# Adding the two halves of an attention accumulator before the scale instead of after it

## The reference, cut to what matters

```python
xf = x.reshape(B, C, N)
f = einsum('kc,bcn->bkn', w1, xf) + b1[None, :, None]     # 16 rows
energy = einsum('bkn,bkm->bnm', f, f)
attention = softmax(energy, axis=-1)
out = einsum('bcm,bnm->bcn', xf, attention)
x = x + out.reshape(B, C, H, W) * 0.1                     # layer 0
...
a = binary_act(x); bw = binarize_weights(weights)         # layer 1
y = conv(a, bw, padding 1)
x = (y - mean) * rsqrt(var + eps) * gamma + beta + x
```

## Time and profile before

| | |
|---|---|
| median of 3 runs | 2013.26 us (2013.1 to 2013.76) |
| the profiled execution | 2013.64 us, its span 2011.8 us (1.84 us lie around it) |
| TensorE busy | 95% |
| DVE, ACT, Pool busy | 80%, 71%, 59% |
| attention, conv | about 54 to 1777 us; 1790.7 us to the end |

### The profile page before, as it was taken

How to read it: one execution, slowest core, us unless ns; L and a number is a source line. 1 busy time by engine, 2 the same in 40 slices (tenths; PEclk the granted TensorE clock), 3 DMA queues, 4 the chain that set the end, 5 groups by cost and what they waited for, 6 DMA issues and landing times. The chain is left out here.

```text
span 2011.8 us, 40245 instructions
## 1 busy us (share of the span) xinstructions
PE 1921.0 (95%) x15232; PEld 1655.3 (82%) x15232; DVE 1600.5 (80%) x2145; ACT 1425.8 (71%) x2794; POOL 1185.0 (59%) x849
## 2 busy tenths in 40 slices
PE   6999999999999999999999999999999999979990
PEld 2799899998889889998899989989999999844440
DVE  6777888888887888888788888888888887647778
ACT  5777777778777777778777777787777777633326
POOL 4555555558755555668655555577555556277750
PEclk7899999999999999999999999999999999989995
DMA  6111101012111111122111110111101102442019
GB/s 215 35 50 60 58 32 40 26 63 73 56 47 60 60 39 31 32 74 93 58 53 60 35 40 22 56 56 53 32 29 31 31 30 76 158 162 110 0 42 375
DMA packets 58279, 133.55 MB, mean 66 GB/s; under 512 B 9329, under 2 KB 9329, under 8 KB 57585
## 3 DMA queue, kind: packets, MB, share of 16 engines
q1 hardware_dynamic: 58096, 131.10, 19.2%
HBM read 84.48 MB, written 33.62 MB: 59 GB/s over the span
## 5 line engine op out<-in xcount | busy, mean ns | idle before, releaser
L724 POOL CAST Ph<-P 128x1024 fp32r<-128x1024 f32 x496 | 715.3, 1442 | 655.6 <-ACT P L497 655.6
L590 DVE TENSOR_REDUCE nb<-scw 128x1 f32<-128x512 f32 (+1 forms) x988 | 680.7, 689 | 271.3 <-PE scw L399 264.4
L508 ACT ACTIVATE scw<-scw,nb 128x512 f32<-128x512 f32 (+1 forms) x988 | 656.1, 664 | 338.1 <-DVE nb L590 337.9
L417 PE MATMUL accb<-Ph,xh 64*128 64x512 f32 x2048 | 809.5, 395 | 1.4 <-ACT tb L518 1.3
L417 PE MATMUL acct<-Ph,xh 64*128 64x512 f32 x2048 | 807.3, 394 | 0.0
L417 PE MATMUL accb<-Ph,xl 64*128 64x512 f32 x2048 | 801.2, 391 | 0.0
L417 PE MATMUL acct<-Ph,xl 64*128 64x512 f32 x2048 | 796.4, 389 | 0.0
L600 DVE TENSOR_TENSOR Pl<-P,Ph 128x1024 fp32r<-128x1024 f32 x512 | 671.9, 1312 | 23.5 <-ACT Ph L502 17.8
L417 PE MATMUL acct<-Pl,xh 64*128 64x512 f32 x2048 | 635.4, 390 | 0.0
L417 PE MATMUL accb<-Pl,xh 64*128 64x512 f32 x2048 | 632.5, 388 | 0.0
L497 ACT ACTIVATE P<-ee 128x1024 f32<-128x1024 f32 x512 | 526.2, 1028 | 64.2 <-PE ee L390 39.4
(11 more groups left out here) (120 smaller groups left out, 1391.0 us busy)
## 6 DMA issues: line engine op xcount, KB each, us to landing
wk<-xt SPq DMA_DIRECT2D x32, 512.0 KB, 3.8
xres<-x SPq DMA_DIRECT2D x32, 512.0 KB, 3.9
x<-xres SPq DMA_DIRECT2D x32, 512.0 KB, 2.8
R<-rd SPq DMA_DIRECT2D x32, 256.0 KB, 3.2
xn<-x SPq DMA_DIRECT2D x16, 512.0 KB, 11.8
xr<-x SPq DMA_DIRECT2D x16, 512.0 KB, 11.2
out<-xr SPq DMA_DIRECT2D x16, 512.0 KB, 3.4
An<-x SPq DMA_DIRECT2D x14, 512.0 KB, 5.0
```

The costliest lines, as they stand in the source:

```text
L417: return pe.matmul(to[:, :], w[rows, g * GM + k, c * 128:(c + 1) * 128], p[rows, s, k * QC:(k + 1) * QC], start=g == 0 and i == 0, stop=g ...
L508: nc.scalar.activation(to, to, ACT.Exp, bias=nb[:, t % 2, w:w + 1], accum_out=bsum[:, t % 2, w:w + 1]).then_inc(bsum_done, 1)
L590: nc.vector.tensor_reduce(nb[:, t % 2, w:w + 1], of, AX.X, ALU.max, negate=True).then_inc(nmax_done, 1)
L724: nc.gpsimd.tensor_copy(Ph[:, e % RP, :], P[:, e % 2, :]).then_inc(ph_done, 1)
```

## The change

For each chunk and half c, ACT still copies `acc_b` to `tb`. DVE now waits for that copy, adds it to `acc_t` straight from PSUM and writes the sum to `tc` (`join`, in the place of `scale_top`). Pool then multiplies `tc` by R once (`scale`) and adds it to x (`add_x`): four Pool operations to a chunk where there were six, at steps 1, 4, 8, 12 (or 2, 5, 11, 13). The waits follow: DVE's operation no longer waits for R but for ACT's copy and, before it overwrites `tc`, for `add_x` of the chunk before; ACT's copy, before it overwrites `tb`, waits for DVE's operation of the chunk before instead of `add_x`; the load of R waits for the two scales only.

```diff
@@ -299,7 +298,6 @@
             def load_r(t):
                 sp.wait_ge(rd_out, 64 * (t + 1))
                 if t >= 1:
-                    sp.wait_ge(top_done, CT * t)
                     sp.wait_ge(scaled, CT * t)
                 sp.dma_start(R[:], rd.rearrange("(o n) -> o n", o=1).to_broadcast([128, QC])).then_inc(r_in, 16)
 
@@ -514,7 +512,7 @@
                 else:
                     act.wait_ge(av_done, 2 * G * (t + 1))
                 if t > 0:
-                    act.wait_ge(x2_done, CT * (t - 1) + c + 1)
+                    act.wait_ge(top_done, CT * (t - 1) + c + 1)
                 nc.scalar.copy(tb[:, c, :], acc_b[c][:]).then_inc(bot_done, 1)
 
             def copy_f(s, bank):
@@ -600,15 +598,15 @@
                 nc.vector.tensor_tensor(Pl[:, e % RP, :], P[:, e % 2, :], Ph[:, e % RP, :].bitcast(F32),
                                         ALU.subtract).then_inc(pl_done, 1)
 
-            def scale_top(t, c):
-                dve.wait_ge(r_in, 16 * (t + 1))
+            def join(t, c):
+                dve.wait_ge(bot_done, CT * t + c + 1)
                 if c == 0:
                     dve.wait_ge(acc_done, 2 * (t + 1))
                 else:
                     dve.wait_ge(av_done, 2 * G * (t + 1))
                 if t > 0:
-                    dve.wait_ge(joined, CT * (t - 1) + c + 1)
-                nc.vector.tensor_tensor(tc[:, c, :], acc_t[c][:], R[:], ALU.mult).then_inc(top_done, 1)
+                    dve.wait_ge(x2_done, CT * (t - 1) + c + 1)
+                nc.vector.tensor_tensor(tc[:, c, :], acc_t[c][:], tb[:, c, :], ALU.add).then_inc(top_done, 1)
 
             def row_max(t):
                 dve.wait_ge(nmax_done, unit_count(SU * (t + 1) - 1))
@@ -672,7 +670,7 @@
                 for s in HEAD_HL.get(u, ()):
                     split_f(s)
                 if g == 0 and t >= 1:
-                    scale_top(t - 1, 1)
+                    join(t - 1, 1)
                 if u < UH:
                     block_max(2 * u, wide[u % 3][:])
                 elif u < NG:
@@ -680,7 +678,7 @@
                 if 0 <= e - 1 < NG:
                     lower(e - 1)
                 if g == G - 1 and t >= 0:
-                    scale_top(t, 0)
+                    join(t, 0)
                 if UH <= u < NG:
                     block_max(2 * u + 1, sc[1])
                 if g == 7 and 0 <= t + 1 < NT:
@@ -698,7 +696,7 @@
                     c = g
                     nc.vector.tensor_reduce(al[:, c:c + 1], xn[:, c, 0:TAPS * C], AX.X, ALU.add,
                                             apply_absolute_value=True).then_inc(al_done, 1)
-            scale_top(NT - 1, 1)
+            join(NT - 1, 1)
 
         @block.gpsimd
         def _(pool):
@@ -723,20 +721,15 @@
                     pool.wait_ge(av_done, 2 * (e - RP + 1))
                 nc.gpsimd.tensor_copy(Ph[:, e % RP, :], P[:, e % 2, :]).then_inc(ph_done, 1)
 
-            def scale_bottom(t, c):
+            def scale(t, c):
                 pool.wait_ge(r_in, 16 * (t + 1))
-                pool.wait_ge(bot_done, CT * t + c + 1)
-                nc.gpsimd.tensor_tensor(tb[:, c, :], tb[:, c, :], R[:], ALU.mult).then_inc(scaled, 1)
-
-            def join(t, c):
+                pool.wait_ge(top_done, CT * t + c + 1)
+                nc.gpsimd.tensor_tensor(tc[:, c, :], tc[:, c, :], R[:], ALU.mult).then_inc(scaled, 1)
+
+            def add_x(t, c):
                 pool.wait_ge(scaled, CT * t + c + 1)
-                pool.wait_ge(top_done, CT * t + c + 1)
-                nc.gpsimd.tensor_tensor(tb[:, c, :], tb[:, c, :], tc[:, c, :], ALU.add).then_inc(joined, 1)
-
-            def add_x(t, c):
-                pool.wait_ge(joined, CT * t + c + 1)
                 pool.wait_ge(xres_in[t % 2], 16 * (t // 2 + 1))
-                nc.gpsimd.tensor_tensor(xres[:, t % 2, c, :], tb[:, c, :], xres[:, t % 2, c, :],
+                nc.gpsimd.tensor_tensor(xres[:, t % 2, c, :], tc[:, c, :], xres[:, t % 2, c, :],
                                         ALU.add).then_inc(x2_done, 1)
 
             for h in range(2 * XG):
@@ -748,13 +741,11 @@
                     round_p(e)
                 part = None
                 if t >= 1:
-                    part = {k: i for i, k in enumerate((2, 5, 8, 11, 13, 15) if t % CH == 0 else (1, 3, 6, 9, 12, 15))}.get(g)
+                    part = {k: i for i, k in enumerate((2, 5, 11, 13) if t % CH == 0 else (1, 4, 8, 12))}.get(g)
                 if part in (0, 1):
-                    scale_bottom(t - 1, part)
-                if part in (2, 4):
-                    join(t - 1, part // 4)
-                if part in (3, 5):
-                    add_x(t - 1, part // 5)
+                    scale(t - 1, part)
+                if part in (2, 3):
+                    add_x(t - 1, part - 2)
                 h = split_at(*divmod(n - 1, G))
                 if h is not None:
                     lower_x(h)
@@ -767,8 +758,7 @@
                     pool.wait_ge(signed, CT * (k + 1))
                     transform_unit(nc, pads[k], V[k], v_done)
             for c in range(CT):
-                scale_bottom(NT - 1, c)
-                join(NT - 1, c)
+                scale(NT - 1, c)
                 add_x(NT - 1, c)
 
 
```

More of the change, by code:

```diff
@@ L177, in attention @@
         scaled = sem("scaled")
-        joined = sem("joined")
         e_done = sem("e_done")
```

## The result

The changed kernel takes 2050.14 us (median of 4 runs, 2048.16 to 2051.55), the kernel before 2013.18 in the same comparison: a ratio of 1.0183, 95% interval 1.0165 to 1.0201. The profiled execution took 2050.09 us, its span is 2048.2, 36.4 longer than the span before.

A forecast was written before the change was run, and what follows sets the result against it. TensorE, 95% busy, was taken as the bound, losing time only where made to wait. The terms 30.6 + 16.2 - 8.5 - 3.9 = +34.4 us gave a forecast of 2048 us, range 2026 to 2063.

The forecast's parts named there:

- The joins: At 30 chunk ends, DVE's joins wait for ACT's copies, so TensorE starts c = 1 1.02 us later: +30.6 us.
- What is late next: In step 1, `lower` behind the second join overlaps Pool's cast, delaying TensorE's second scan 0.54 us, 30 times: +16.2 us.
- the replay: Chunk 9's end retimed with the joins, using gaps from the profile; `lower` starts 0.27 us inside Pool's cast.
- Pool: `add_x` of c = 0 moves from step 9 to 8, ending step 11's wait: 23 chunks times 0.37, -8.5 us.
- The tail: After the last attention matmul, Pool runs four operations instead of seven before the convolution: -3.9 us.
- The clock: Clock taken as 1.00; its rival: idling at each boundary sets off a clock fall, 62 us more, 2110 us, chance 0.02.
- the other rivals: Step 1's wait absent, 2031 us (0.16); step 2 also delayed, 2063 (0.10); step 11 keeps its wait, 2056 (0.06).
- the not-slower case: Joins covered beside TensorE's first half step, only gains stay: 2001 us, chance 0.07; faster below 0.41 us a boundary.

The follow-up runs named there:

- the three kernels with the maximum moved: Step 15's `block_max` put ahead of DVE's c = 0 operation: changed kernel 2016.43 us; also `lower` ahead of second join 2003.33; kernel before, `add_x` in steps 8 and 14, 2004.69.
- the wait-alone run: Kernel before, with only a wait added so that DVE's `scale_top` also waits for ACT's copy: 2062.04 us, ratio 1.0242.

## Why the prediction was right, point by point

The forecast was 2048, the measurement 2050.1.

- **The joins** (+30.6 forecast, +25.6 measured). The mechanism is as told, and adding the wait alone makes it. The size was 0.2 us a boundary too large, in two places. ACT's second copy starts 0.67 after the start of its sum, not the 0.78 that I took from the earlier trace rows: there the sum's accumulator read was followed by nothing, since the copy waited for Pool. And TensorE restarts 0.06 after the join's end (618.33 to 618.39), not 0.14. One sign did not come: the gap ahead of c = 1 was to be near 1.3 us, 1.42 from the scan's start to the matmul's, and is 0.94. Part of the wait lies ahead of c = 0 instead, which the prediction took as hidden inside this wait. That is right for the sum, since the start of c = 1 hangs on the second join alone (0.06 behind its end at every boundary), but it made me miss what was left when that wait was taken away (the three kernels with the maximum moved).
- **What is late next** (+16.2 forecast, +17.7 measured). `lower` starts 0.25 inside the cast where the replay said 0.27, and is held to 1.08 behind its end. Moving `lower` ahead takes this term away and nothing else of its size; that the overlap alone makes it is worked out from the rows, not run. In the Trainium skill, SBUF — State Buffer, section "SBUF: two separate sides", GpSimd and a VectorE operation with two SBUF inputs take a pair of ports in turn, for a whole instruction; the 1.87 us here and the 1254 ns of the tiny operation with `add_x` in step 9 agree with that.
- **Pool** (-8.5 forecast, -9.7 measured). Step 11 is free, in nearly all chunks; one number in Pool's list gives it and takes it away, in either kernel. What I costed at nothing, the Pool parts that now fall into steps which also split x (chunks 7, 15, 23), came to 2.1 us in steps 7 and 8.
- **The tail** (-3.9 forecast, -3.9 measured): four operations, and the convolution's first matmul 17.87 us behind the last energy matmuls instead of 21.77. No run varied it by itself.
- **The clock.** The mean from 60 to 1740 us is 1.00, with waits of TensorE's weight loads up to 1.5 us and of its matmuls up to 1.1 in the list: no fall, so that rival is out. It is a mean: the first stretch, 60 to 64 us, still shows 0.50, but that is in chunk 0, ahead of every boundary.
- The terms come to +29.6 where +34.4 was forecast. That the total is close all the same is luck: some 7 us lie elsewhere, which the prediction had put at nothing, 4.6 of them in the steps named above and the rest in chunk 0 and in tenths that no run here isolates.
- Of the other rivals, the not-slower case stands against the wait-alone run. Its point, 0.41 us a boundary, was right in kind: with `lower` and the maximum moved, the boundary costs about what it did before the change, and the kernel with the joins is indeed faster than the one before it, though 6.8 us slower than that one with two `add_x` moved.

## What to carry to other kernels

An operation in order on an engine that has idle time can still be on the path: what counts is what queues behind it, and here two hand-overs from ACT to DVE at each of 30 boundaries cost more than removing 64 Pool operations could give. Work that needs no late input (here `lower`) belongs ahead of such a wait, but a move must be followed for every reader of what it pushes back (the maximum moved ahead pushed back the join that TensorE's first half step wanted). Ask of a long list of off-path operations not how many there are but what each overlaps: two `add_x` moved by one step, with all six operations kept, took 17 us off the kernel before.

## What the runs showed of the hardware that was not expected

TensorE's restart behind a DVE operation is not one number: in the changed kernel its matmul started 0.06 us after the join's end at c = 1 and 0.26 at c = 0, at nearly every boundary, and 0.26 at c = 0 again in the kernels with the maximum moved. What makes the difference is not shown. The other observation was in the prediction for one chunk, and the runs switch it on and off in most: a 128x4 operation on DVE takes 0.15 us alone and up to 1.27 when a 128x512 Pool operation has started just ahead of it, so the smallest instruction of the chunk cost some 0.36 us of TensorE's time there.
